# First norm and projections of a decoder kernel regrouped by four tiles, with expert weights, input and output moved in other pieces

## What is computed

```python
x = x + L0_attn(layernorm(x), ...)                # gated slot attention, 16 heads
x = x + L0_xattn(layernorm(x), ctx, ctx, ...)     # mLSTM
x = x + L0_ffn(layernorm(x), ...)                 # attention with rope + mixture of experts
x = x + L1_attn(layernorm(x), ...)                # causal attention + memories
x = x + L1_xattn(layernorm(x), ctx, ctx, mask, ...)
x = x + L1_ffn(layernorm(x), ...)                 # mixture of experts
```

```python
g    = log_sigmoid(h @ Wf1 @ Wf2)
beta = sigmoid(h @ Wb)
gate = h @ Wg1 @ Wg2 + bg2
```

## Time and profile before

| | us |
|---|---|
| runs | 7500.79, 7512.69, 7509.68 |
| median | 7509.68 |
| profiled execution | 7506.52 |
| its span, first to last instruction | 7504.7 |
| mean granted TensorE clock | 0.966 |

### The profile page before, as it was taken

How to read it: one execution, slowest core, us unless ns; L and a number is a source line. 1 busy time by engine, 2 the same in 40 slices (tenths; PEclk the granted TensorE clock), 3 DMA queues, 4 the chain that set the end, 5 groups by cost and what they waited for, 6 DMA issues and landing times. The chain is left out here.

```text
span 7504.7 us, 126616 instructions
## 1 busy us (share of the span) xinstructions
PE 6600.1 (88%) x46376; PEld 4909.5 (65%) x46376; DVE 4601.9 (61%) x9389; ACT 3926.7 (52%) x8401; POOL 1441.4 (19%) x1769
## 2 busy tenths in 40 slices
PE   4699999999989999999999997878799989887999
PEld 3477676676766767667776766766555556675555
DVE  2477777777777777777777775667422247665222
ACT  2467667676676766766666674536311124343111
POOL 0122222222222222222222221321000000010000
PEclk9999999999999999999999998879899999998999
DMA  0000000000000000000000000000211100001111
GB/s 24 9 4 2 6 5 2 6 6 4 2 6 5 2 6 5 2 6 5 4 3 6 5 2 21 16 10 2 63 35 34 34 20 2 17 15 52 39 43 48
DMA packets 64169, 107.57 MB, mean 14 GB/s; under 512 B 11856, under 2 KB 34960, under 8 KB 62608
## 3 DMA queue, kind: packets, MB, share of 16 engines
q1 hardware_dynamic: 63504, 98.86, 4.3%
HBM read 94.34 MB, written 4.49 MB: 13 GB/s over the span
## 5 line engine op out<-in xcount | busy, mean ns | idle before, releaser
L137 ACT ACTIVATE ffn0b_sl<-PSA 128x512 f32<-128x512 f32 x136 | 81.3, 598 | 629.4 <-PE PSA L68 629.4
L137 ACT ACTIVATE ffn1b_sl<-PSA 128x512 f32<-128x512 f32 x112 | 67.0, 598 | 518.3 <-PE PSA L68 518.3
L68 PE MATMUL PSA<-H0T,ffn0b_WG 128*128 128x512 f32 x544 | 257.5, 596 | 12.7 <-DMA ffn0b_WU<-in_e_up 12.7
L77 PEld LDWEIGHTS PSA<-ffn0b_WD,ffn0b_hidden 128*128 128x128 f32 x1088 | 206.7, 190 | 85.3 <-issue 64.1
L101 DVE TENSOR_TENSOR ffn0b_up<-PSA,ffn0b_CB 128x512 f32<-128x512 f32 x88 | 60.9, 692 | 326.4 <-PE PSA L68 304.9
L101 DVE TENSOR_TENSOR ffn1b_up<-PSA,ffn1b_CB 128x512 f32<-128x512 f32 x88 | 60.9, 692 | 324.4 <-PE PSA L68 304.8
L77 PE MATMUL PSA<-ffn0b_WD,ffn0b_hidden 128*128 128x256 f32 x1088 | 256.7, 379 | 0.0
L68 PE MATMUL PSA<-H0T,ffn0b_WU 128*128 128x512 f32 x544 | 256.3, 594 | 0.0
L1180 ACT ACTIVATE gsa_caa<-PSA,gsa_nmxa 128x128 f32<-128x128 f32 x256 | 90.7, 366 | 295.8 <-DVE gsa_nmxa L977 295.8
L1109 ACT ACTIVATE gsa_cab<-PSA,gsa_nmxb 128x128 f32<-128x128 f32 x256 | 90.7, 366 | 287.4 <-DVE gsa_nmxb L842 287.4
L1265 POOL TENSOR_TENSOR gsa_ssa<-gsa_ssa,gsa_neghalf 128x4 f32<-128x4 f32 x64 | 88.2, 1378 | 735.2 <-DVE gsa_ssa L889 735.2
(11 more groups left out here) (678 smaller groups left out, 20289.2 us busy)
## 6 DMA issues: line engine op xcount, KB each, us to landing
gsa_wa<-in_w_heads SPq DMA_DIRECT2D x16, 512.0 KB, 3.6
ffn0b_CB<-ffn0b_cw_rows SPq DMA_DIRECT2D x32, 256.0 KB, 3.1
ffn1b_CB<-ffn1b_cw_rows SPq DMA_DIRECT2D x32, 256.0 KB, 3.2
X<-in_x SPq DMA_DIRECT2D x1, 4096.0 KB, 14.6
mlstm_CX<-in_ctx SPq DMA_DIRECT2D x32, 128.0 KB, 2.0
cross_CX<-in_ctx SPq DMA_DIRECT2D x32, 128.0 KB, 2.1
out_x<-X SPq DMA_DIRECT2D x1, 4096.0 KB, 13.5
ffn0b_CB<-ffn0b_cw_rows SPq DMA_DIRECT2D x16, 224.0 KB, 2.9
```

What stands on the lines that cost most here:

```text
L68: last = nc.tensor.matmul(bank[:, :], w[:, c, k * 128:(k + 1) * 128], HT[:, c, g * 512:(g + 1) * 512], start=(c == 0), stop=(c == 1))
L77: last = nc.tensor.matmul(PS[4 + j][:, 0:256], hidden[step % HIDDEN][:, j * 128:(j + 1) * 128], WD[:, k, :], start=(k == 0), stop=(k == ch ...
L137: nc.scalar.activation(sl[step % 2][:, :], PS[step % 2][:, :], ACT.Silu).then_inc(silu_by_act, 1)
```

## The change

Four things are changed.

- The opening block is gone. `prep` issues the identity, its three weights and X in eight pieces of four tiles, each piece with a semaphore of its own.
- `prep` has no loop any more: it is written out for 8 groups of four tiles. PE transposes group g + 1 before it multiplies group g; moments of group g + 1 stand before the normalization of group g on DVE. Transposed tiles go from PSUM straight to XT by ACT, the two low-rank products are made 512 columns at a time, and ACT takes Sigmoid for BETA in place of exp on ACT and add and reciprocal on DVE. ACT's program of the stage has two table loads, one ahead of its first copy and one ahead of its first Sigmoid.
- The expert weights have buffers that live through two stages. The loads of the first set are issued in `ffn0a` behind its own loads, those of the second in `cross`, between its small loads and the context rows. `moe` issues none and waits for all three at its first `widen`.
- In `ffn1b` SP stores X by groups of 512 rows once they are added, group g - 1 behind the CB loads of group g, the last at the end of the stage. The closing block only waits for the eight stores.

On PE, at the start of `prep`: before, the loop body of one tile (run 32 times).

The diff, cut to the parts that the prediction speaks of:

```diff
 def moe(...)
-                pe.wait_ge(loads, 32)
+                pe.wait_ge(fetched, 48)
                 widen(0)
                 widen(1)
                 pe.wait_ge(cw_turned_by_act, 1)
-                pe.wait_ge(down_loads, 16)
...
-                nc.sync.dma_start(WG[:, :, :], io[prefix + "_gate"]).then_inc(loads, 16)
-                nc.sync.dma_start(WU[:, :, :], io[prefix + "_up"]).then_inc(loads, 16)
+                def put(g):
+                    out, x_stored = store
+                    sp.wait_ge(added_by_dve, g + 1)
+                    nc.sync.dma_start(out[g * 512:(g + 1) * 512, :].rearrange("(i p) d -> p i d", p=128), X[:, g * 1024:(g + 1) * 1024].rearrange("p (i d) -> p i d", d=256)).then_inc(x_stored, 16)
...
-                nc.sync.dma_start(WD[:, :, :], io[prefix + "_down"]).then_inc(down_loads, 16)
...
+                    if store and g >= 1:
+                        put(g - 1)
+                if store:
+                    put(GROUPS - 1)
 def prep(...)
+                def turn(g):
+                    pe.wait_ge(normed_by_dve, g + 1)
+                    if g >= 2:
+                        pe.wait_ge(turned_by_act, 2 * (g - 1))
                     for c in range(2):
+                        for j in range(4):
+                            last = nc.tensor.transpose(PS[2 * (g % 2) + c][:, j * 128:(j + 1) * 128], xn[g % 2][:, j, c * 128:(c + 1) * 128], IDENT[:, :])
...
+                def project(g):
+                    pe.wait_ge(turned_by_act, 2 * (g + 1))
+                    if g >= 1:
+                        pe.wait_ge(lowrank_by_act, 2 * g)
                     for c in range(2):
+                        last = nc.tensor.matmul(PS[4][:, :], WF1[:, c, :], XT[:, c, g * 512:(g + 1) * 512], start=(c == 0), stop=(c == 1))
...
+                    for j in range(4):
+                        i = 4 * g + j
+                        for c in range(2):
+                            last = nc.tensor.matmul(PS[6 + g % 2][:, j * 16:(j + 1) * 16], XT[:, c, i * 128:(i + 1) * 128], WB[:, c, :], start=(c == 0), stop=(c == 1))
...
+                pe.wait_ge(identity, 16)
+                turn(0)
+                pe.wait_ge(weights, 48)
+                for g in range(GROUPS):
+                    if g + 1 < GROUPS:
+                        turn(g + 1)
+                    project(g)
...
+                for g in range(GROUPS):
+                    moments(g)
+                    if g >= 1:
+                        normalize(g - 1)
+                normalize(GROUPS - 1)
...
+                fetch(0)
+                nc.sync.dma_start(IDENT[:, :], io["ident"]).then_inc(identity, 16)
...
+                for g in range(1, GROUPS):
+                    fetch(g)
 def cross(...)
                 nc.sync.dma_start(MK8[:, :], io["mask"]).then_inc(loads, 16)
+                nc.sync.dma_start(EG[:, :, :], io["e1_gate"]).then_inc(fetched, 16)
+                nc.sync.dma_start(EU[:, :, :], io["e1_up"]).then_inc(fetched, 16)
+                nc.sync.dma_start(ED[:, :, :], io["e1_down"]).then_inc(fetched, 16)
                 for n in range(TILES):
```

More of the change, by code:

```diff
@@ L10, with moe @@
 AX = mybir.AxisListType
-def moe(nc, io, X, PS, IDENT, shared, name, prefix, chunks, gated):
+def moe(nc, io, X, PS, IDENT, shared, name, prefix, chunks, gated, store=None):
     ctx = ExitStack()
@@ L194, in signal @@
         def signal(name):
-            signals.append(nc.alloc_semaphore(name))
+            signals.append(nc.alloc_semaphore("prep_" + name))
             return signals[-1]
[L198 to L202, removed]
-        XT, F1T, G1T, BETA = shared
+        GROUPS = 8
+        XT, F1T, G1T, BETA = shared
+        stats = sb("stats", [128, 32, 6])
+        mv = sb("mv", [128, 32, 2])
+        vare = sb("vare", [128, 32])
+        rstd = sb("rstd", [128, 32])
+        xn = [sb(f"xn{k}", [128, 4, 256]) for k in range(2)]
         WF1 = sb("wf1", [128, 2, 128])
@@ L242, in _ @@
                     for c in range(2):
-                        nc.tensor.matmul(PS2[:, 0:128], WF1[:, c, :], xTf[:, c, :], start=(c == 0), stop=(c == 1))
-                    for c in range(2):
-                        last = nc.tensor.matmul(PS3[:, 0:128], WG1[:, c, :], xTf[:, c, :], start=(c == 0), stop=(c == 1))
-                    last.then_inc(prep_lowrank_by_pe, 1)
+                        last = nc.tensor.matmul(PS[5][:, :], WG1[:, c, :], XT[:, c, g * 512:(g + 1) * 512], start=(c == 0), stop=(c == 1))
@@ new lines, in moments @@
+                def moments(g):
+                    dve.wait_ge(x_in[g], 16)
+                    for i in range(4 * g, 4 * g + 4):
+                        nc.vector.bn_stats(stats[:, i, :], X[:, i * 256:(i + 1) * 256]).then_inc(stats_by_dve, 1)
+                    for i in range(4 * g, 4 * g + 4):
+                        dve.wait_ge(stats_by_dve, i + 1)
+                        dve.sem_inc(dve_passed, 1)
+                        last = nc.vector.bn_aggr(mv[:, i, :], stats[:, i, :])
+                    last.then_inc(moments_by_dve, 1)
@@ new lines, in normalize @@
+                def normalize(g):
+                    dve.wait_ge(rstd_by_pool, g + 1)
+                    if g >= 2:
+                        dve.wait_ge(turned_by_pe, g - 1)
+                    for j in range(4):
+                        i = 4 * g + j
+                        last = nc.vector.tensor_scalar(xn[g % 2][:, j, :], X[:, i * 256:(i + 1) * 256], mv[:, i, 0:1], rstd[:, i:i + 1], ALU.subtract, ALU.mult)
+                    last.then_inc(normed_by_dve, 1)
+                for g in range(GROUPS):
+                    moments(g)
+                    if g >= 1:
+                        normalize(g - 1)
@@ new lines, in _ @@
+                pool.wait_ge(setup_by_pool, 1)
+                for g in range(GROUPS):
+                    pool.wait_ge(moments_by_dve, g + 1)
+                    pool.sem_inc(pool_passed, 1)
+                    nc.gpsimd.tensor_scalar(vare[:, 4 * g:4 * g + 4], mv[:, 4 * g:4 * g + 4, 1:2].rearrange("p i o -> p (i o)"), 1e-5, None, ALU.add).then_inc(variance_by_pool, 1)
+                    pool.wait_ge(variance_by_pool, g + 1)
+                    nc.gpsimd.tensor_tensor(rstd[:, 4 * g:4 * g + 4], vare[:, 4 * g:4 * g + 4], NEGHALF[:, :], ALU.pow).then_inc(rstd_by_pool, 1)
@@ L3305, in cross, with ffn1b @@
         nc.all_engine_barrier()
-def ffn1b(nc, io, X, PS, IDENT, shared):
-    moe(nc, io, X, PS, IDENT, shared, "ffn1b", "e1", 14, False)
+def ffn1b(nc, io, X, PS, IDENT, shared, store):
+    moe(nc, io, X, PS, IDENT, shared, "ffn1b", "e1", 14, False, store)
 def decoder(nc, io, out):
```

145 lines of the change are left out of this document (60 added, 85 removed).

## The result

The changed kernel takes **7266.49 us** (median of 4 runs, 7260.84 to 7270.76) against 7505.24 us for the kernel before in runs beside it (7486.69 to 7512.69): a ratio of 0.9685, 95% interval 0.9665 to 0.9705.

What follows compares the result with a forecast made beforehand. A chain through all engines bounded the first 273 us; PE would bound the new stage. Terms -205.3 - 11.6 + 10.3 - 10.4 - 10.7 = -227.7 took 7506.52 to 7278.8, median 7282, range 7269 to 7303.

Steps and rivals of the forecast that it cites:

- What bounds: First 273 us: a chain through all engines before the change; PE bounds the new stage at 6.1 us a group.
- `prep`: Start and `prep`: PE-bound groups bring the first DMA of `gsa` to 67.1 us in place of 272.47, -205.3.
- The rule against it: `prep` ramp: transposes don't count as activity for PE's clock, so it stays slow until 22; 0.9 us worse.
- rival 1: `prep`: PE stays at 1.2 GHz throughout, costing 49 us, 7331; chance 0.07.
- `ffn0b`: First mixture: no wait for weights, `widen(2)` then limited by CB's product; -11.6 us (-10.5 to -12.7).
- `ffn1b`: Second mixture: no wait for weights, `widen(2)` then limited by CB's product; -10.4 us (-9.3 to -11.2).
- `cross`: Start of `cross`: second expert set's loads hold the context rows in the queue; +10.3 us (0 to +13.9).
- the third rival: `cross`: context rows are not held by the expert loads; 10.3 us better, 7272; chance 0.08.
- Store: End of kernel: last 512 KB piece issued behind the last add without a barrier; -10.7 us (-9 to -12).
- the second (8 us a group): `prep`: PE is not the bound, a four-engine ring wait closes each group; +15 us, 7297; chance 0.09.
- the fourth: `gsa`: granted less clock after dense work, kernel slower than before; at 0.92 granted, 7539; chance 0.01.
- The fifth: `ffn0b`: CB alone was late, so early weights give nothing; costs 11 us of gain; chance 0.01.

Runs made afterwards that it cites:

- the run with four turns: Against the changed kernel, every transpose of `prep` is issued four times over, same operands and same place; 7294.34 us (one run).
- The run with the context rows first: Against the changed kernel, the second expert set's loads in `cross` are issued behind the first four context rows; 7261.49 us, ratio 0.9681.

## Why the prediction was right, and where it was wrong

- **What bounds.** Right. `prep` was a chain and is now PE's: PE is busy without a wait from 14.8 to 64.8.
- **`prep`.** Predicted -205.3, measured -206.6. The group of 6.1 us came out at 6.05. DVE's 4.3 us a group were over-sized: four like instructions in a row take 1.41, not 4 x 0.43, and DVE's group is about 2.9. That brought turn(1) to 14.80 instead of 15.7, though the second piece, which I had far ahead of DVE, held it 2.30 us. project(0) ends at 23.1 (24.1 predicted), and `gsa` begins at 65.9 (67.1). Between the traces with this `prep` that start moves from 64.3 to 67.1, with the landing of the second piece and the rise of the clock.
- **The rule against it.** The rule that the forecast took from the Trainium skill ("TensorE: Matmul & The Clock Gate", "Part 4: PE-mode transpose") would have made the ramp 0.9 us worse, and rival 1 the whole 49 us. Neither happened, and the run with four turns shows why: transposes alone raised the clock. The falls seen in `prep` all came behind a gap of 1.17 us, which this `prep` doesn't have.
- **`ffn0b`** -10.4 for -11.6, just past the weaker bound of -10.5. The stores landed sooner than assumed (SG is issued at 5164.74, 1.35 us behind the last store's issue, against 2.0), but the first `CB` took 4.8 us from issue to use (5165.13 to 5169.91) where I had 3.1 "at most", a median over many. There is a slip in the sum too: 5378.9 and 3.1 are 5382.0, not 5381.7, so its own steps give -11.3. **`ffn1b`** -9.8 for -10.4, for the same reason (the first `CB` 4.2 us from issue to use).
- **`cross`** +10.2 for +10.3, in part by luck. The first row was turned 22.4 us behind the stage's first DMA where I had 24.1: the three loads landed 4.3 us apart, not 4.6, and the small loads before them 1.3 us sooner than in the trace before. There the row was turned at 13.9, so it came 8.5 later; the other 1.6 us stand behind the row, in work that is the same. Over the eleven traces in which `cross` starts with its own loads the row is turned at 22.2 to 24.1 with the loads ahead (seven) and at 12.6 to 14.3 without (four). The run with the context rows first takes the 10 us back, at 371.18, and the third rival falls.
- **Store** -11.4 for -10.7; the last piece needed 3.3 us, not 4.0.
- **The other rivals.** No wait closes a group of `prep`, so the second (8 us a group) falls. `gsa` had its granted 0.98 as before, so the fourth does. The fifth falls with the -10.4 of `ffn0b`.
- **The sum** of the touched terms was -227.7, and they measure -228.0. That they agree to 0.3 us is luck: single terms are off by up to 1.3 both ways, and in the second trace of the changed kernel the same stretches give -221.3.

The step that failed is the last one, from the sum to the median and its range. The forecast of 7282 is 15.5 us too high. Of these, 8.9 stand between the traces (7278.8 predicted, 7269.92 measured): 0.3 in the touched terms and 8.6 in the stages that nothing touches, for which the sum had no term. The sum put them at nothing because the change touches none of their instructions, and gave them no spread either; they measured -7.4 (`gsa`), -5.0 (`mlstm`), -2.4 (`infini`) and +6.1 (`ffn0a`). The other 6.6 come from "its time is 3.2 below the median of the runs shown, so the median becomes 7282": I carried one execution's distance from a median of three over as if it belonged to the kernel. Of the changed kernel the profiled execution is 3.4 *above* its median.

The same gap is in "The range 7269 to 7303 takes in forecast, rivals 2 and 3": the range was built from the touched terms and had nothing for the rest. `gsa` alone moves by 19 us between traces (4321.6 to 4340.9), and the medians of two measurements of the same changed kernel lie 10.9 us apart; by the second one, 7277.36, the range would have held. With some 10 us to either side for that the range would have begun near 7260. What the earlier trace rows showed and I did not use is the granted clock of 0.98: 2% of 3940 us is a term that need not be the same twice. How much of the 8.6 is such spread, and whether `mlstm`'s 5.0 are an effect of the new `prep`, the runs leave open.

## What to carry to other kernels

Cost a pipelined stage by the engine that is busiest in a group, and use the duration of several like instructions in a row, not four times a single one. Behind a sum of terms put the spread of the part that isn't touched, from two executions of the same kernel, above all where a throttled engine fills most of it. And in the one DMA queue of this kernel loads arrived in the order of issue (context rows turned 22.4 us behind the stage's first DMA with 5376 KB ahead of them, 12.6 without): what the next step needs is issued ahead of what only a later stage needs.

## What the runs showed of the hardware that was not expected

- Transposes alone raised PE's clock: 0.20 us each in 11:15, 0.105 in 17:21, nothing else on the engine.
- Where PE waited 1.17 us in every group, the clock fell to its lower level (granted 0.50) in 4 of 14 groups, for the 3.4 to 3.7 us of the next four records of 512 columns (1.98 otherwise). In 49 groups without the wait it never fell.
- The granted clock reads 1.00 in the ramp too, where transposes took twice their time (11:15 of the run with four turns): in these traces the column shows the falls behind dense work, not the slow start.
- With X in one piece, the next DMA in the queue took 7.89 us to issue; behind one piece of 512 KB the same DMA took 0.49:

```profile
0.76 0.45 SPq L327 DMA_DIRECT2D X<-in_x  x1
1.27 7.89 SPq L328 DMA_DIRECT2D IDENT<-in_ident  x1
```
